# Diagonal attention blocks: once, with a decay product and a subtracted maximum, and a result that stays transposed

## What is computed

```
scores = einsum('bhqd,bhkd->bhqk', qh, k_rec) / sqrt(d)
decay  = exp(-0.01 * abs(t[:, None] - t[None, :]))
attn   = softmax(scores * decay, axis=-1)
out    = einsum('bhqk,bhkd->bhqd', attn, v_rec)      # then @ W_o
```

## Time and profile before

| | |
|---|---|
| time, 3 runs | 2752.46 us median (2750.56 to 2753.69) |
| the profiled execution | 2753.01 us, span 2751.1 us |
| attention stage, steps | about 417 to 2060 us of the span |
| feed stage | about 2106 us to the end |
| PE busy | 2592.5 us (94%) |
| DVE busy | 2308.7 us (84%) |
| ACT busy | 1600.6 us (58%) |
| POOL busy | 971.2 us (35%) |

### The profile page before, as it was taken

One profiled execution on the slowest core, in us unless ns is written; L12 is line 12 of the kernel. 1 busy time (PEld: TensorE's weight loads), 2 busy tenths in 40 slices (PEclk: granted clock), 3 DMA queues, 4 the chain that ended last, 5 costly groups with the idle time before them and its releaser, 6 DMA issues. The chain is left out here.

```text
span 2751.1 us, 44454 instructions
## 1 busy us (share of the span) xinstructions
PE 2592.5 (94%) x15110; PEld 1205.3 (44%) x15110; DVE 2308.7 (84%) x4659; ACT 1600.6 (58%) x2988; POOL 971.2 (35%) x865
## 2 busy tenths in 40 slices
PE   5787669999999999999999999999977999999998
PEld 3333304344344344344344344343323566666665
DVE  5988788888888888888888888888755888888886
ACT  3666507777777777777777777777762222222221
POOL 3666532222122122122122122122131565556664
PEclk9667659999999999999999999999996999999999
DMA  4778864546546536446446446456201111111110
GB/s 153 239 243 257 264 127 82 85 62 91 82 62 92 81 66 95 74 69 96 72 71 95 70 74 95 69 74 92 47 7 39 37 44 42 41 41 43 41 34 18
DMA packets 207074, 238.20 MB, mean 87 GB/s; under 512 B 32256, under 2 KB 150784, under 8 KB 206720
## 3 DMA queue, kind: packets, MB, share of 16 engines
q1 hardware_dynamic: 194560, 218.56, 41.2%
q0 software_dynamic: 3072, 8.39, 1.2%
q10 hardware_dynamic: 9216, 8.39, 0.9%
HBM read 149.79 MB, written 83.89 MB: 85 GB/s over the span
## 5 line engine op out<-in xcount | busy, mean ns | idle before, releaser
L856 DVE CUSTOM_DVE_ANT_0 unread<-max_ps,toeplitz_sb 128x1024 bf16<-128x1024 f32 x1024 | 1218.5, 1218 | 212.9 <-PE max_ps L689 207.6
L817 ACT ACTIVATE probs<-score_ps 128x512 f32<-128x512 f32 x2048 | 1111.5, 598 | 431.0 <-PE score_ps L722 287.3
L689 PE MATMUL max_ps<-k_low,q_low 96*128 96x512 bf16 x2048 | 712.9, 391 | 27.5 <-DVE ident_bf L847 17.9
L651 POOL TENSOR_TENSOR probs<-probs,up_probs 128x512 f32<-128x512 f32 x256 | 336.3, 1314 | 610.0 <-ACT up_probs L821 610.0
L750 PE MATMUL pv_ps<-probs,v 128*32 128x512 f32 x4096 | 545.5, 605 | 3.3 <-POOL probs L651 3.3
L714 PE MATMUL score_ps<-q_up,k_up 99*128 99x512 bf16 (+3 forms) x1280 | 408.6, 320 | 5.3 <-ACT probs L817 4.5
L722 PE MATMUL score_ps<-q_low,k_low 99*128 99x512 bf16 (+3 forms) x1280 | 406.2, 318 | 5.2 <-ACT probs L817 4.5
L1284 PE MATMUL gu_ps<-wgu_t,turned 128*128 128x512 f32 (+1 forms) x768 | 314.4, 559 | 0.6 <-DVE hid L1445 0.6
L657 POOL DMA_DIRECT2D attn<-out_n x64 | 48.8, 763 | 694.8 <-DVE out_n L920 671.4
L714 PEld LDWEIGHTS score_ps<-q_up,k_up 99*128 99x128 bf16 x1280 | 123.8, 97 | 357.3 <-ACT probs L817 340.8
L689 PEld LDWEIGHTS max_ps<-k_low,q_low 96*128 96x128 bf16 x2048 | 193.3, 99 | 146.0 <-DVE row_max L856 68.3
(11 more groups left out here) (145 smaller groups left out, 3186.3 us busy)
## 6 DMA issues: line engine op xcount, KB each, us to landing
splits<-parts SPq DMA_DIRECT2D x128, 384.0 KB, 2.7
q_low<-splits SPq DMA_DIRECT2D x192, 128.0 KB, 4.4
k_low<-splits SPq DMA_DIRECT2D x192, 128.0 KB, 7.2
q_up<-splits SPq DMA_DIRECT2D x192, 128.0 KB, 9.8
k_up<-splits SPq DMA_DIRECT2D x192, 128.0 KB, 12.7
v_padded<-v_out SPq DMA_DIRECT2D x64, 256.0 KB, 3.7
v<-v_padded SPq DMA_DIRECT2D x32, 512.0 KB, 14.8
x_in<-in_L_attn_x SPq DMA_DIRECT2D x16, 512.0 KB, 5.3
```

The costliest lines, as they stand in the source:

```text
L651: nc.gpsimd.tensor_tensor(probs[:, g % PROBS, :, at:at + P], probs[:, g % PROBS, :, at:at + P], up_probs[:, g % 2], ALU.add).then_inc(diag ...
L689: mm = pe.matmul(max_ps[:, i % 2, half * HALF:(half + 1) * HALF], low[0][u][0:KROWS, h, qb * P:(qb + 1) * P], low[1][u][0:KROWS, h, half * ...
L817: nc.scalar.activation(probs[:, g % PROBS, h, :], score_ps[:, i % 2, :], ACT.Exp).then_inc(exp_done, 1)
L856: nc.vector.tensor_tensor_reduce(unread[:, i % 2, :], max_ps[:, i % 2, :], toeplitz[:, at:at + S], 1.0, -3.0e38, ALU.mult, ALU.max, row_ma ...
```

## The change

The diagonal block is made once, without masks and without the maximum rows, in `side_ps` from the low operands (`diagonals`), one step earlier than before. VectorE multiplies it by exp(-0.02 max(0, k - q)) as it reads it, into `diag` (`decay_diagonal`). GpSimd subtracts the maximum (`shift_diagonal`) from `shift`, a copy of the maxima in every partition: the maxima are also turned whole, written to DRAM, and loaded with a broadcast of 1 MB for each half unit. ScalarE exponentiates `diag` straight into its 128 columns of `probs` (`diagonal_exp`), and leaves the outermost blocks out of its own 512 columns. `out_t`, four buffers now, stays transposed: the columns of v beyond the 16 values are all ones, so that the sums come out in 16 rows for each head. SyncE moves them next to the values (`move_sums`), GpSimd raises 128 x 512 of them to the power -1 and multiplies by them (`normalise`), and SyncE stores the rows (`store_out`). Both halves of a unit are normalised in the next unit, between its diagonals 3 and 12. `feed_stage` loads the result transposed and no longer turns it, so its pipeline is one step shorter. v has two buffers rather than four, and the buffers of the FP4 rounding of the weights lie in the operands of the first unit.

```diff
@@ attend_stage, SyncE @@
+        def load_shift(unit, hf):
+            sp.wait_ge(max_stored, 16 * (unit + 1))
+            if unit > 0:
+                sp.wait_ge(diag_shifted, 2 * DIAG * (unit - 1) + DIAG * (hf + 1))
+            sp.dma_start(shift[:, hf], t["max_whole"].rearrange("(h c) q -> h (c q)", c=TILES)[
+                :, hf * HALF:(hf + 1) * HALF].unsqueeze(0).broadcast_to([P, UH, HALF])).then_inc(shift_loaded[hf], 16)
+
+        def move_sums(unit, hf):
...
+            for h in range(UH):
+                sp.dma_start(inverse[h * VW:h * VW + HD, hf, :],
+                             out_t[h * VW + HD:(h + 1) * VW, n % OUTS, :]).then_inc(sums_moved[hf], 16)
+
+        def store_out(b, u, hf):
+            n = 2 * (UNITS * b + u) + hf
+            sp.wait_ge(out_normal, n + 1)
+            for h in range(UH):
+                sp.dma_start(t["attn_t"][b, u * UH + h, :, hf * HALF:(hf + 1) * HALF],
+                             out_t[h * VW:h * VW + HD, n % OUTS, :]).then_inc(out_stored[n % OUTS], 16)
...
+            if unit > 0:
+                load_shift(unit, 1)
+                sp.wait_ge(pv_done, STEPS * unit)
+            if not (last and u == UNITS - 1):
+                load_v(b if u < UNITS - 1 else b + 1, (u + 1) % UNITS)
+            if unit > 0:
+                move_sums(unit - 1, 1)
+                store_out(*before, 0)
+                store_out(*before, 1)
+            move_sums(unit, 0)
+            if not (last and u == UNITS - 1):
                 load_max_rows(unit + 1, (u + 1) % UNITS)
+                load_shift(unit + 1, 0)
@@ attend_stage, GpSimd @@
-        def add_diagonal(b, u, g):
...
-            nc.gpsimd.tensor_tensor(probs[:, g % PROBS, :, at:at + P], probs[:, g % PROBS, :, at:at + P],
-                                    up_probs[:, g % 2], ALU.add).then_inc(diag_added, 1)
...
+        def shift_diagonal(unit, g):
...
+            nc.gpsimd.tensor_tensor(diag[:, g % 2], diag[:, g % 2], shift[:, hf, :, at:at + P],
+                                    ALU.subtract).then_inc(diag_shifted, 1)
+
+        def normalise(unit, hf):
+            n = 2 * unit + hf
...
+            pool.wait_ge(sums_moved[hf], 16 * UH * (unit + 1))
+            nc.gpsimd.tensor_tensor(inverse[:, hf, :], inverse[:, hf, :], minus_one[:].broadcast_to([P, HALF]),
+                                    ALU.pow).then_inc(inverted, 1)
+            pool.wait_ge(inverted, n + 1)
+            nc.gpsimd.tensor_tensor(out_t[:, n % OUTS, :], out_t[:, n % OUTS, :], inverse[:, hf, :],
+                                    ALU.mult).then_inc(out_normal, 1)
+
+        def unit_steps(unit):
             for g in range(DIAG):
...
+                shift_diagonal(unit, g)
+            if unit > 0:
+                normalise(unit - 1, 0)
+                normalise(unit - 1, 1)
             for g in range(TILES + DIAG, STEPS):
...
+                shift_diagonal(unit, g)
...
+        normalise(UNITS * B - 1, 0)
+        normalise(UNITS * B - 1, 1)
@@ attend_stage, TensorE @@
+            pe.transpose(turned_max, max_parts[:].rearrange("p t n -> p (t n)"), ident_bf[:])
+            pe.transpose(turned_whole, row_max[:, unit % 2], w["ident"][:]).then_inc(max_turn_ready, 1)
...
             if is_diagonal(g):
-                at = score_ps[:, i % 2, turn - q0:turn - q0 + P]
-                pe.matmul(at, low[1][u][:, h, ks], low[0][u][:, h, ks], start=True, stop=False)
-                mm = pe.matmul(at, ident_bf[:], unserved[:], start=False, stop=True)
                 turn += P
...
-                mm = pe.matmul(side_ps[:, h, :], up[1][u % 2][:, h, ks], up[0][u % 2][:, h, ks],
+                mm = pe.matmul(side_ps[:, h, :], low[1][u][0:KROWS, h, ks], low[0][u][0:KROWS, h, ks],
...
-        def turn_out(n, turned_maxima=0):
...
-                    if h == 1 and is_diagonal(g):
-                        up_diagonals(b, u, g)
+                    if h == 1 and is_diagonal((g + 1) % STEPS) and not (last and g == STEPS - 1):
+                        diagonals(*steps_on(b, u, g))
@@ attend_stage, ScalarE @@
-            nc.scalar.activation(probs[:, g % PROBS, h, :], score_ps[:, i % 2, :], ACT.Exp).then_inc(exp_done, 1)
...
+            nc.scalar.activation(probs[:, g % PROBS, h, first:end], score_ps[:, i % 2, first:end],
+                                 ACT.Exp).then_inc(exp_done, 1)
...
+            act.wait_ge(diag_shifted, diagonals_before(unit, g + 1))
+            nc.scalar.activation(probs[:, g % PROBS, :, at:at + P], diag[:, g % 2], ACT.Exp).then_inc(diag_exp_done, 1)
@@ attend_stage, VectorE @@
-            nc.vector.tensor_tensor(up_probs[:, g % 2], side_ps[:], up_limit[:].unsqueeze(1).broadcast_to([P, UH, P]),
-                                    ALU.min).then_inc(up_limited, 1)
+            nc.vector.tensor_copy(max_whole[:], turned_whole).then_inc(max_turn_copied, 1)
...
+            if n >= 2:
+                dve.wait_ge(diag_exp_done, n - 1)
+            nc.vector.tensor_tensor(diag[:, g % 2], side_ps[:], diag_decay[:].unsqueeze(1).broadcast_to([P, UH, P]),
+                                    ALU.mult).then_inc(diag_decayed, 1)
...
-        def invert_sums(n):
...
-        def normalise(n):
@@ feed_stage @@
-    TURN_ATTENTION = 0
-    PROJECT = NORM = 1
...
+    PROJECT = NORM = 0
...
+            sp.dma_start(attn_in[i % 4][:], t["attn_t"][b, :, :, tokens].rearrange(
+                "(k h) d s -> (h d) k s", k=DC)).then_inc(tile_loaded[i % 4], 16)
...
-                mm = pe.matmul(out_ps[:, 0:D], turned[i % 2][:, k, :], w["wo_g"][:, b, k, :],
+                mm = pe.matmul(out_ps[:, 0:D], attn_in[i % 4][:, k, :], w["wo_g"][:, b, k, :],
...
-        def turn_attention(b, i):
```

More of the change, by code:

```diff
@@ L545, in attend_stage @@
     up_loaded = [sem(f"up_loaded{i}") for i in range(2)]
-    v_loaded = [sem(f"v_loaded{i}") for i in range(UNITS)]
+    v_loaded = [sem(f"v_loaded{i}") for i in range(2)]
     max_rows_loaded = sem("max_rows_loaded")
@@ L636, in _ @@
             step(B - 1, u, True)
+        move_sums(UNITS * B - 1, 1)
+        store_out(B - 1, UNITS - 1, 0)
+        store_out(B - 1, UNITS - 1, 1)
+        for i in range(OUTS):
+            sp.wait_ge(out_stored[i], 16 * UH * 2 * UNITS * B // OUTS)
     @block.gpsimd
@@ L654, in store @@
[L654 to L660, removed]
+        pool.wait_ge(minus_ones_set, UNITS + 2)
+        nc.gpsimd.memset(minus_one[:], -1.0).then_inc(minus_ones_set, 1)
+        nc.gpsimd.memset(inverse[:], 1.0).then_inc(minus_ones_set, 1)
@@ L661, in unit_steps @@
+        def unit_steps(unit):
             for g in range(DIAG):
-                add_diagonal(b, u, g)
-            if not first:
-                store(*steps_back(b, u, 0, 1)[:2], 1)
-            store(b, u, 0)
+                shift_diagonal(unit, g)
+            if unit > 0:
+                normalise(unit - 1, 0)
+                normalise(unit - 1, 1)
             for g in range(TILES + DIAG, STEPS):
-                add_diagonal(b, u, g)
-        for u in range(UNITS):
-            unit_steps(0, u, u == 0)
@@ L671, in _ @@
-        for b in range(1, B):
-            for u in range(UNITS):
-                unit_steps(b, u, False)
-        store(B - 1, UNITS - 1, 1)
-        pool.wait_ge(out_stored, 16 * 2 * UNITS * B)
+                shift_diagonal(unit, g)
+        for unit in range(UNITS * B):
+            unit_steps(unit)
+        normalise(UNITS * B - 1, 0)
+        normalise(UNITS * B - 1, 1)
     @block.tensor
@@ L931, in unit_steps @@
                         maxima(ahead[0], ahead[1], ahead[2] + i)
-                    if not first and (g, i) == (6, 0):
-                        invert_sums(2 * unit - 1)
-                    if not first and (g, i) == (6, 1):
-                        normalise(2 * unit - 1)
                     if not last and (g, i) in SPLIT_AT:
@@ L1158, in sem @@
         return st.enter_context(nc.semaphore(name))
-    attn_in = [sb(f"attn_in{i}", [P, D], F32) for i in range(4)]
+    attn_in = [sb(f"attn_in{i}", [P, DC, P], F32) for i in range(4)]
     res_in = [sb(f"res_in{i}", [P, D], F32) for i in range(4)]
-    turned = [sb(f"turned{i}", [P, 2 * DC, P], F32) for i in range(2)]
+    turned = [sb(f"turned{i}", [P, DC, P], F32) for i in range(2)]
     x1 = [sb(f"x1_{i}", [P, D], F32) for i in range(TILES)]
@@ L1538, in constants @@
     ahead = np.arange(TOEPLITZ)[None, :] - (S - P) - np.arange(P)[:, None]
-    before = np.arange(P)[None, :] < np.arange(P)[:, None]
-    large = np.float32(-2.0 ** 100)
-    unserved = np.where(before, large, np.float32(0))
+    behind = np.arange(P)[:, None] - np.arange(P)[None, :]
     return {
@@ L1548, in constants @@
         "toeplitz": np.exp(-2.0 * decay * np.maximum(ahead, 0)).astype(np.float32),
-        "unserved": (unserved.view(np.uint32) >> 16).astype(np.uint16),
-        "up_limit": np.where(before, np.float32(3.0e38), large),
+        "diag_decay": np.exp(-2.0 * decay * np.maximum(behind, 0)).astype(np.float32),
     }
```

268 lines of the change are left out of this document (127 added, 141 removed).

## The result

The changed kernel takes 7281.5 us against 2753.1 us: 2.645 times as long (95% interval 2.641 to 2.650). The direction and the mechanism were as forecast; the size was not, 5880 us were said and the range ended at 6300.

A forecast was written before the change was run, and what follows sets the result against it. TensorE was taken to bound the kernel before, GpSimd's powers after: thirty cycles of 149 us within 5204 us to the attention stage's end, plus 671 for what follows, about 5880 us; range 2590 to 6300.

The forecast's parts named there:

- the mechanism: Attention stage: GpSimd's in-order powers delay subtraction 12, hence ScalarE, TensorE and the next unit's maxima; chance 0.58.
- the term P: Length of one GpSimd power over 128 x 512, twice a unit: 59.6 us, from 115 ns for each further element.
- the prediction's sum: Attention cycles, tail and later stages add to 5880 us; each us of a power's length counts 64 times.
- the 27 us: Attention cycle, from the second normalisation's end to the next power: 24.5 us of chain plus 2.5 for TensorE's clock.
- my own signs of being wrong: Power outside 35 to 66 us; cycle not 2P plus 25-30; broadcast beyond 6 us holding the subtraction; feed tiles unchanged.
- my 24.5 us: From the second normalisation's end through SyncE's loads, broadcast, subtractions and steps to the next power, before the clock's 2.5 us.
- TensorE's gain: Attention stage: fewer diagonal matmuls and no result turns shorten a unit by 3.9 us, to 47.3.
- rival A: Powers up to 10 us are hidden under steps 4 to 11: 2621 us, range 2590 to 2690; chance 0.24.
- its cover: Feed stage: VectorE's 1.09 us of slack lets TensorE's saving of two transposes a tile, 18 us in all, show.
- the 0.28: Feed stage: us saved per tile by dropping two transposes, 18 us over 64 tiles.

The follow-up runs named there:

- the half powers: Changed kernel with GpSimd's power taken of only 256 of the 512 columns, the others multiplied by the sums (wrong result): 4671.6 us in a single run.
- kernel without powers: Changed kernel with GpSimd's power and its wait removed, so the result is multiplied by the sums (wrong result): 2637.5 us, 0.958 of the kernel before.
- the few powers: Changed kernel with a unit's different sums gathered, inverted once on GpSimd and spread through DRAM; SyncE stores after loading the next maxima: 2853.5 us, 1.037 of before.
- the transposes put back: Changed kernel without GpSimd's powers, with two unused matmuls per diagonal score tile and two unused transposes per feed tile added back: 2725.8 us.

## Why the prediction was wrong, point by point

**The step that failed** is the term P, the power's length: 59.6 us forecast, 81.9 measured, and even the 77 that I named as the upper end by the shortest 128 x 1 is 5 us short. I took the median of the one-element row, 662 ns, and so 115 ns an element. The rate is 159. A difference of two small rows, read in two stages, was multiplied by 508: the 113 ns that the one-element power takes longer in the feed stage than alone became 19 of the 22 us that P lacks, and the sum counts them 64 times. The trace of before had the better value, the 558 ns of a power with VectorE idle beside it; I read 558 to 734 as scatter, and it was two conditions. With P = 81.9 the prediction's sum gives 5877 + 64 x 22.3 = 7304 us, 0.3% from the measured time. The range failed for a second reason: I let a long loop be faster than the short rows, down to 35 us, and cut the other side at 66 though the rows themselves reached 77. Even the 7000 us for P = 77 lie below the measured time.

**The mechanism was right.** The cycle is 2(P + 1.31) + 27: 193.4 us by the formula, 193.9 in the trace. Each us of P costs 64: 64.0 between the changed kernel and the half powers.

That the 27 us come out to 0.2 is in part luck. One of my own signs of being wrong came true: the broadcast takes 8.9 us and not 6, and it is what the first subtraction waits for. So the stretch is my 24.5 us, 2.1 for the late broadcast and 0.6 for the steps after it, where I had put 2.5 for the clock. The clock did fall, twice a cycle: it was 0.50 and 0.58 from 1028 to 1036 us, and 0.63 and 0.52 from 1048 to 1056. The first time is hidden behind the broadcast, and the second has at most the 0.6. Of the other signs, P lay outside 35 to 66, and the feed tiles hardly changed.

**TensorE's gain was right in size.** 3.9 us a unit were forecast and 3.56 came. The kernel without powers was to take 2621 us and took 2637. The diagonal steps were held by VectorE as said: where it makes a product, its operations follow each other with hardly a gap.

```profile
750.34 0.69 DVE L941 TENSOR_TENSOR diag<-side_ps,diag_decay 128x512 f32<-128x512 f32 x1
750.96 1.23 DVE L906 CUSTOM_DVE_ANT_0 unread<-max_ps,toeplitz_sb 128x1024 bf16<-128x1024 f32 x1
...
753.25 0.69 DVE L941 TENSOR_TENSOR diag<-side_ps,diag_decay 128x512 f32<-128x512 f32 x1
```

The products start 2.91 us apart here, where 2.95 were forecast.

**The limit at which rival A holds was wrong.** I had the second half's sums moved 16 us into the unit and so P up to 10 us hidden. In the kernel without powers the loads begin at 746.6 and the second product runs at 778.5, 32 us in, after 18.7 us of waiting for the DMA. I counted issues and one landing, and not what stood in the queue before them, although the last of the loads took 12.7 us to land in the kernel before:

```profile
k_up<-splits SPq DMA_DIRECT2D x192, 128.0 KB, 12.7
```

Subtraction 12 is due some 36 us in, which leaves an estimated 3 us for the second power, and no run tried that length. A power of 10 us there would have run into subtraction 12 as the few powers did.

**The feed stage was wrong too.** I called VectorE's 1.09 us of idle time its cover. That time is a wait inside a loop through all engines, and when two transposes go, VectorE's and GpSimd's operations lie otherwise against each other. One VectorE operation, first in the kernel before, then without the powers (min/median/max ns):

```profile
L1427 DVE TENSOR_SCALAR normed<-x,mean_var,rstd x64: 403/404/1755, 2111.1 to 2698.6; 128x256 f32<-128x256 f32 x64
```

```profile
L1439 DVE TENSOR_SCALAR normed<-x,mean_var,rstd x64: 404/936/1756, 1996.4 to 2582.2; 128x256 f32<-128x256 f32 x64
```

The median is 0.53 us longer. The length of this operation follows its overlap with a subtraction of 128 x 704 on GpSimd (L1028, in the kernel before L1000): with 0.1 us of overlap it takes 0.40 us, with 0.8 us 0.94, which is so for 51 of the 64 without the powers, and with 1.6 us 1.76. With the transposes put back the overlap is 0.1 us again for most, and its mean is 491 ns. VectorE's idle time falls from 1.09 to 0.41 us a tile, and TensorE, which waits for no other engine in the kernel before, now waits for GpSimd. Without the powers, from 2200 to 2500 us (us in total, times, longest us):

```profile
DVE hid L1457 <- ACT silu L1337: 12.9, 32, 0.4
...
PEld hid_ps L1287 <- POOL hid L1029: 5.3, 32, 0.2
```

These 0.17 us a tile are most of the 0.21 that are missing from the 0.28. That the overlap is what makes TensorE wait is argued: no run took GpSimd's operation away. The Trainium skill's "GPSIMD Engine Reference" says in section 1 that GpSimd's SBUF interfaces are shared with VectorE and contend with its instructions in a 2-port perf mode or with two SBUF inputs. The trace agrees that the two engines hold each other up; which of the two cases this operation is, no run shows.

On the price of the power, the same page's figure of about 2.6 cycles an element (section 3.1), an estimated 1.1 us for 512, is near the subtraction (1.28 us) and a factor of some 70 below the power (81.9 us); the page measured it on an add. One slip of mine is small: the 1.31 us that I called a product's was an addition's, and the product takes 1.26.

## What to carry to other kernels

A rate that comes from the difference of two short instructions must not be multiplied by hundreds: measure the shape itself, or take the range from the extremes of both rows with nothing cut off. When a short row scatters, look at what ran beside the short and the long ones before taking the median. Before an operation of unknown price goes to the idle engine, count its elements, and count distinct values: here 1/32 of them were enough. And a small DMA can take the time of what stands before it in its queue; where a result is awaited in the same unit, give it another queue.

## What the runs showed of the hardware that I had not expected

- A power on GpSimd costs 155 to 160 ns an element and partition at every length from 2 to 512, for the exponents -1 and -0.5 and on ones and other values.
- VectorE's reciprocal of 128 x 128 from SBUF takes 945 ns, when 128 x 16 takes 230, 128 x 44 takes 367 and 128 x 88 takes 692: 5 to 7 ns an element.
- Four DMAs of 2 KB behind 4.5 MB of loads in SyncE's queue landed some 15 us after their last issue, and still 9.5 us after it on GpSimd's queue; on SyncE's queue without the loads in front the median is 1.7 us.
- A power of one element takes 0.55 to 0.57 us with VectorE idle and 0.66 to 0.73 beside VectorE's work in the feed stage, while powers of four and of 512 elements took as long beside VectorE's work as without it. What sets the single element apart is open.
- One VectorE operation took from 0.40 to 1.76 us, longer by as much as it overlapped with a subtraction on GpSimd.
